# Layer 3: adding the scan's groups of states on POOL itself instead of by accumulating DMAs

## The reference

```python
def step(state, inp):                       # for each of the 256 rows
    d_t, u_t, b_t, c_t = inp
    state = jnp.exp(d_t[..., None] * A) * state + (d_t * u_t)[..., None] * b_t[:, None, :]
    y_t = jnp.einsum('bdn,bn->bd', state, c_t)      # sum over the 16 states n
    return (state, y_t)
y = ys + x * D
y = y * silu(z)
out = y @ out_proj_w.T
```

## Time and profile before

| | |
|---|---|
| device time, median of three | 3774.03 us |
| device time of the profiled execution | 3774.03 us |
| its span | 3772.1 us |
| layer 3's steps, first to last start | 2237.29 to 3668.00 us, 15 steps |
| TensorE busy | 2966.5 us, 79% |
| VectorE busy | 2471.2 us, 66% |
| ScalarE busy | 1790.8 us, 47% |
| POOL busy | 281.5 us, 7% |
| POOL's accumulating DMAs | 96 of 512 KB (7.2 us to landing), 32 of 256 KB (3.8 us) |

### The profile page before, as it was taken

The page is one execution under the profiler, slowest core; times in us unless marked ns, Lnnn a source line. Parts: engine busy times, 40 slices in busy tenths (PEclk is TensorE's granted clock), DMA queues, the critical chain, the costliest instruction groups (busy, mean ns, idle before and its releaser), DMA issues. The chain is left out here.

```text
span 3772.1 us, 60296 instructions
## 1 busy us (share of the span) xinstructions
PE 2966.5 (79%) x19822; PEld 2407.2 (64%) x19822; DVE 2471.2 (66%) x7020; ACT 1790.8 (47%) x4073; POOL 281.5 (7%) x339
## 2 busy tenths in 40 slices
PE   3888888888899898998655737777777777777777
PEld 2766776767788787887544625555555555555555
DVE  2555455555666666666677267777777777777776
ACT  1222222224555555555334345555555555555555
POOL 0000000000000000000011121111111111111111
PEclk9888778779999999999767857777777777777777
DMA  5000000000000000000200113333333333333334
GB/s 164 0 0 0 0 0 0 0 0 1 0 0 0 0 0 0 0 0 0 62 10 8 53 56 85 85 85 85 85 85 85 80 87 79 82 84 85 85 85 107
DMA packets 84918, 162.31 MB, mean 43 GB/s; under 512 B 18856, under 2 KB 44080, under 8 KB 84784
## 3 DMA queue, kind: packets, MB, share of 16 engines
q0 software_dynamic: 20480, 62.93, 9.3%
q1 hardware_dynamic: 63104, 97.36, 7.7%
q10 hardware_dynamic: 1200, 0.27, 0.1%
HBM read 92.59 MB, written 9.21 MB: 27 GB/s over the span
## 5 line engine op out<-in xcount | busy, mean ns | idle before, releaser
L966 ACT ACTIVATE b_neg<-b_neg,b_nmax 128x128 f32<-128x128 f32 (+1 forms) x512 | 228.5, 447 | 272.7 <-DVE b_nmax L1074 271.5
L2424 DVE TENSOR_TENSOR_SCAN d_state<-w,d_state 128x1024 f32<-128x1024 f32 x128 | 289.2, 2280 | 6.1 <-issue 6.1
L2159 ACT ACTIVATE d_probs<-l_bank,w_b 128x256 f32<-128x256 f32 x512 | 210.7, 469 | 155.7 <-PE l_bank L2007 153.3
L2007 PE MATMUL l_bank<-xnT,w_w 128*128 128x256 f32 x1024 | 245.1, 382 | 12.0 <-ACT d_probs L2159 12.0
L2018 PE MATMUL l_bank<-w_w,d_probs 128*128 128x128 f32 x2048 | 252.7, 276 | 0.0
L2018 PEld LDWEIGHTS l_bank<-w_w,d_probs 128*128 128x128 f32 x2048 | 244.9, 192 | 11.7 <-ACT d_probs L2159 5.3
L607 ACT ACTIVATE a_hT<-l_bank,lnb,lnw 128x128 f32<-128x128 f32 x128 | 46.5, 468 | 431.5 <-PE l_bank L553 431.5
L1970 PE MATMUL l_bank<-w 8*128 8x256 f32 x1024 | 117.1, 610 | 168.0 <-DVE d_qk L2410 138.3
L1062 DVE SCALAR_TENSOR_TENSOR b_gated<-b_th,l_bank 128x256 f32<-128x256 f32 x256 | 107.5, 420 | 209.0 <-ACT b_th L960 204.7
L518 PE MATMUL l_bank<-a_vmem,a_memT 128*128 128x128 f32 x768 | 187.7, 368 | 71.4 <-ACT a_h L602 71.4
L1984 PE MATMUL l_bank<-w 9*128 9x256 f32 x1024 | 200.3, 669 | 35.3 <-ACT w L2099 17.8
(11 more groups left out here) (406 smaller groups left out, 7336.4 us busy)
## 6 DMA issues: line engine op xcount, KB each, us to landing
d_bct<-l_bc SPq DMA_DIRECT2D x132, 512.0 KB, 6.5
d_state<-d_state POOLq DMA_DIRECT2D x96, 512.0 KB, 7.2
d_state<-d_state POOLq DMA_DIRECT2D x32, 256.0 KB, 3.8
x_sorted<-x SPq DMA_DIRECT2D x1, 2176.0 KB, 15.5
w<-in_L_ffn_w_dram SPq DMA_DIRECT2D x1, 2048.0 KB, 10.2
w_w<-in_L_ffn_W_dram SPq DMA_DIRECT2D x1, 2048.0 KB
c2e_xg<-x_sorted SPq DMA_DIRECT2D x16, 128.0 KB, 2.3
y_sorted<-c2e_yo SPq DMA_DIRECT2D x16, 128.0 KB, 1.8
```

The source lines that it names most:

```text
L966: done = nc.scalar.activation(neg[:, h % RP, cols], neg[:, h % RP, cols], ACT.Exp, bias=nmax[:, h % RP, a:a + 1], scale=-1.0, accum_out=to ...
L2007: done = nc.tensor.matmul(bank[:, b, i * T:(i + 1) * T], w.w1[:, e, k * P:(k + 1) * P], x1T[:, :], start=True, stop=True)
L2159: done = v.activation(hid[:, e % 2, k, :], bank[:, b, i * T:(i + 1) * T], ACT.Gelu, bias=w.b1[:, e, k:k + 1])
L2424: done = v.tensor_tensor_scan(group, dA[i][:, g % (NG - 1), :, :].rearrange("p m t -> p (m t)"), group, 0.0, ALU.mult, ALU.add)
```

## The change

The DMAs of `add_group` and of the halves become additions that POOL executes itself: `nc.gpsimd.tensor_tensor` with the same slices. The waits for landings and their semaphores go. A `drain` of POOL stands behind each group. `sum_ready` is raised once, by the last addition, so VectorE waits for n + 1 in place of 32 (n + 1). The order of the steps on every engine is as before; on the other engines no instruction changes.

```diff
--- before.py
+++ after.py
@@ -1857,8 +1857,6 @@
         dA_ready = sem("dA_ready")
         scanned = sem("scanned")
         cstate_ready = sem("cstate_ready")
-        group_added = sem("group_added")
-        pool_step = sem("pool_step")
         sum_ready = sem("sum_ready")
         ym_ready = sem("ym_ready")
         s_in_psum = sem("s_in_psum")
@@ -2227,13 +2225,10 @@
 
                     def add_group(g):
                         pool.wait_ge(cstate_ready, NG * n + g + 1)
-                        pool.sem_inc(pool_step, 1)
-                        if g > 1:
-                            pool.wait_ge(group_added, 16 * CI * ((NG - 1) * n + g - 1))
-                            pool.sem_inc(pool_step, 1)
                         for i in range(CI):
-                            pool.dma_start(st[i][:, 0:SG, :], st[i][:, SG * g:SG * (g + 1), :], accum_op=ALU.add)\
-                                .then_inc(group_added, 16)
+                            nc.gpsimd.tensor_tensor(st[i][:, 0:SG, :], st[i][:, 0:SG, :],
+                                                    st[i][:, SG * g:SG * (g + 1), :], ALU.add)
+                        nc.gpsimd.drain()
 
                     norm_power(nc, c, s, n + 1)
                     add_group(1)
@@ -2241,10 +2236,9 @@
                     residual(n + 1, 1 - par)
                     add_group(2)
                     add_group(3)
-                    pool.wait_ge(group_added, 16 * CI * (NG - 1) * (n + 1))
-                    pool.sem_inc(pool_step, 1)
                     for i in range(CI):
-                        pool.dma_start(st[i][:, 0:2, :], st[i][:, 2:SG, :], accum_op=ALU.add).then_inc(sum_ready, 16)
+                        done = nc.gpsimd.tensor_tensor(st[i][:, 0:2, :], st[i][:, 0:2, :], st[i][:, 2:SG, :], ALU.add)
+                    done.then_inc(sum_ready, 1)
                     inner_power(2 * n + 2)
 
         @block.sync
@@ -2511,7 +2505,7 @@
                     add_expert(4)
                     first_part(n + 1)
                     add_expert(5)
-                    dve.wait_ge(sum_ready, 16 * CI * (n + 1))
+                    dve.wait_ge(sum_ready, n + 1)
                     for i in range(CI):
                         v.scalar_tensor_tensor(out=ym[:, i, :], in0=xs[:, par, i, :], scalar=w.skip[:, i:i + 1],
                                                in1=st[i][:, 0, :], op0=ALU.mult, op1=ALU.add)
```

## The result

The changed kernel takes 3814.0 us (median of four, 3808.8 to 3819.3) against 3773.7: ratio 1.011, 95% interval 1.0084 to 1.0137, 40 us slower. The forecast was 3803.

A forecast was written before the change was run, and what follows sets the result against it. No engine is full; each step is a relay between VectorE, TensorE and ScalarE. Holding of 3.42 + 5.32 = 8.74 us less 6.9 of waits gives about +1.8 a step, +29 over 16: 3774 + 29 = 3803 us, range 3743 to 3832.

The forecast's parts named there:

- POOL's durations: POOL additions estimated from L2214 with VectorE's fixed part: 2.41 us for 1024 columns, 1.29 us for 512.
- the reverse case: POOL's tiny power L2218 took 1.24 us instead of 710 ns, waiting until VectorE's two-SBUF-input L2358 ended.
- Rival 1: Nothing blocks; only VectorE's wait at L2516 goes, 1.8 us a step gained, 3745 us; chance 0.22.
- The walk: Following 15 steps through POOL's additions and VectorE's waits: +1.8 us a step on average, +29 us over 16.
- rival 2: POOL keeps hold over back-to-back adds, +3.5 us a step; smaller version, strict turns, +2.9; 3820 to 3831 us; chance 0.23.
- Group 2: POOL's two adds hold the router's L182 by 1.93 us and L2486 by 1.49: VectorE 3.42 us late.
- Group 3: With the halves, 7.40 us of POOL adds hold the rotary products from L2337 by 5.32 us in all.
- Group 1 at nothing: Adds beside the four L2417 cost 0, covered by the 6.0 us wait before L2464; 1.2 us of cover left.
- The sum per step: 8.74 us of holding minus 6.9 us of waits given back: last expert sum +1.84 us later.
- TensorE stalls too: In group 3's stretch, expert sum 3 is late and TensorE, at most two experts ahead, stalls; no separate size given.
- Rival 3: Additions block VectorE but are short, 1.8 to 2.3 us: -21 to +21 us, around 3776; chance 0.17.
- The two low points of the prediction's scale: Total change if POOL's 1024-column add were shorter: +12 us at 2.20 us, -21 us at 1.80 us.

The follow-up runs named there:

- the run with the filled stall: Changed kernel plus 7 extra 128x256 matmuls on TensorE just before its wait for expert sum 3: 3804.0 us, ratio 1.0064.
- the run with group 3: Kernel before with only group 3 and the halves added on POOL, groups 1 and 2 still by DMA: ratio 0.9981.

## Why the prediction was right

The direction and its mechanism were right; that the size came so near was partly luck, as the sum per step shows.

- *POOL's durations.* Predicted 2.41 and 1.29 us, measured 2.354 and 1.299. The fixed part taken from VectorE served well.
- *The additions are serialized with VectorE's two-input work.* Right, and it gave the sign. The inference from the reverse case was confirmed directly: L182 1.88 instead of 0.18 us. Rival 1 and its 3745 us came about (3748.1) where POOL did not read.
- *Who gets the next turn.* The walk let a few products slip between POOL's additions. In the trace it is one product, one addition; two passed only during POOL's drain. These are the strict turns of rival 2's smaller version, but not at its price of 2.9 us a step: at full clock the step grew by 1.0 to 1.2. Its larger version, POOL keeping hold over two additions, falls: L182 was held once, not for 4.3 us.
- *Group 2.* 3.42 us of holding predicted; measured 1.71 (L182) and 1.30 (L190), 3.0 together. The second was not L2486 with its two inputs but the cast just before it, which has one and can be held as well. I had not counted casts.
- *Group 3.* 5.32 predicted, 0.92 + 2.16 + 1.05 + 1.08 = 5.2 measured.
- *Group 1 at nothing.* Right: the cover shrank to 1.67 us, and moving this group alone changed nothing.
- *The sum per step.* Here the terms were off and partly cancelled. The last expert sum should have moved by 1.84 us; at full clock, in the step shown, it moved by 0.9 and the step by 1.0, as the holding was 0.5 us less (8.2 instead of 8.74) and the waits gave back 7.3 us instead of 6.9. What the sum lacked is the clock: "TensorE stalls too" stood in it, with no price for what follows the stall. In 9 of 15 steps the granted clock was 0.5 after it. By the run with the filled stall that is 1.05 us a step on average, 1.75 where it happens; the 2.1 by which the two kinds of step differ is more, as they are not the same steps. So +1.22 stands where +1.8 was forecast, and +1.05 where nothing was.
- *Rival 3*, short additions: the duration was outside its 1.8 to 2.3 us, though only by 0.05. The two low points of the prediction's scale are off by its own factor: 4.6 times 16 makes +14 at 2.20 us and -16 at 1.80, not +12 and -21. The forecast does not rest on them.

Not shown: why 6 of the 15 stalls of equal length were not followed by the lower clock. In the kernels before and after, the clock is also at 0.5 around every change of step, until 41 to 44 us into the next one. That part is common to both: from the last expert sum to the step's end it is 11.4 us in either.

## What to carry to other kernels

Before moving elementwise work to POOL, list what VectorE executes beside it: here each product with two SBUF inputs waited for the end of the POOL addition that it met, however small it was, and so did a cast. A row of tiny products beside long additions was the worst neighbour, a VectorE that was idle or read PSUM the best. Ask of each moved piece alone whether it has cover; here one third cost everything, one third nothing, and the smallest piece by itself was worth 0.8%. The parts did not add up: +1.6 us a step apart, +2.3 together. And price a stall of TensorE with the clock that follows it.

## What the runs showed of the hardware that was not expected

- VectorE and POOL, both with instructions waiting, alternate one by one: products of 0.22 us took 2.38, then 1.28 and 1.30 us.
- POOL's writes hold the cast L190 (0.62 instead of 0.175 us) and the selections (0.89 instead of 0.29), but neither the router's nor the rotary products with two inputs (0.176 and 0.218 us, unchanged).
- A TensorE stall of 3.06 us is followed in 9 of 15 steps by a granted clock of 0.5 for 3.4 or 6.8 us; the one of 1.05 us in the run with group 3 was in none of 15.
